# Cross-attention and expert layer on one core: the expert phase written out as a straight program of 136 slots in place of a hardware loop of eight slots a turn

## What is computed

```
x = x + attention(layernorm(x), ctx, ctx)     # causal linear attention, 16 heads, elu+1 features
x = x + ffn(layernorm(x))
ffn: h = relu(x @ W1 + b1); logits = h @ W2 + b2; sel = argmax(softmax(logits))   # 8 experts
     out[token] = x[token] @ expert_W[sel] + expert_b[sel]
```

## Time and profile before

| | us |
|---|---|
| median of three runs | 1158.4 |
| the three runs | 1156.0, 1158.4, 1158.63 |
| span of the profiled execution | 1158.5 |
| of it the second phase, from the first row load (961.3) | 197.2 |
| of it from the first to the last output DMA's issue on POOL | 184.5 |

### The profile page before, as it was taken

One profiled execution on the slowest core, in us unless ns is written; L12 is line 12 of the kernel. 1 busy time (PEld: TensorE's weight loads), 2 busy tenths in 40 slices (PEclk: granted clock), 3 DMA queues, 4 the chain that ended last, 5 costly groups with the idle time before them and its releaser, 6 DMA issues.

```text
span 1158.5 us, 39374 instructions
## 1 busy us (share of the span) xinstructions
PE 1044.3 (90%) x15828; PEld 727.5 (63%) x15829; DVE 843.8 (73%) x1739; ACT 562.7 (49%) x945; POOL 587.0 (51%) x682
## 2 busy tenths in 40 slices
PE   2989999999999999999999999999999626999996
PEld 1666666666666666666667666666667414666664
DVE  2688887887888887878878788888877643555554
ACT  2544544454555544554455545445444114666664
POOL 4144444544444455554555444544444444777766
PEclk9989999999999999999999999999999857999999
DMA  3823333333333333333334333333322014666664
GB/s 104 241 75 93 94 93 94 93 93 93 94 93 95 97 97 97 101 101 100 107 104 120 97 93 93 93 93 93 93 76 76 30 51 138 193 190 184 195 185 135
DMA packets 88601, 127.11 MB, mean 110 GB/s; under 512 B 13693, under 2 KB 67584, under 8 KB 88320
## 3 DMA queue, kind: packets, MB, share of 16 engines
q1 hardware_dynamic: 75392, 89.98, 30.1%
q0 software_dynamic: 13056, 34.90, 7.9%
HBM read 73.03 MB, written 36.06 MB: 94 GB/s over the span
## 4 chain that ended last, share of the span: by engine, by line
PE 23%; issue 23%; POOL 18%; DMA 13%; SPq 7%; ACT 5%; DVE 4%; DVEq 0%; POOLq 0%; ACTq 0%
DMA x_res<-in_x 8%; PE b_a L808 8%; POOL buckets L409 7%; PE b_b L1014 6%; SPq L338 5%; POOL x_res L433 3%; DMA stage<-buckets 2%; DMA out<-stage 2%; PE b_b L855 2%; PE b_a L1005 2%; ACT x2n L494 2%; POOL row L419 2%; PE b_a L803 2%; PE b_b L813 2%; ACT x2T L506 1%
## 5 line engine op out<-in xcount | busy, mean ns | idle before, releaser
L581 DVE TENSOR_TENSOR stage<-b_s,causal 128x1024 f32<-128x1024 f32 x192 | 226.1, 1219 | 47.6 <-PE b_s L835 37.1
L461 POOL DMA_INDIRECT out<-stage x136 | 136.6, 1005 | 59.2 <-issue 30.2
L409 POOL DMA_INDIRECT buckets<-row,place x128 | 140.8, 1100 | 34.6 <-issue 34.6
L1014 PE MATMUL b_b<-we_sb,x3T 128*128 x544 | 150.5, 400 | 0.0
L808 PE MATMUL b_a<-xnT,wq_sb 128*128 128x512 f32 x256 | 128.0, 624 | 7.4 <-ACT x2T L506 5.1
L539 ACT ACTIVATE x3n<-stage 128x256 f32<-128x256 f32 x136 | 81.5, 599 | 88.4 <-DMA stage<-buckets 83.8
L813 PE MATMUL b_b<-wo_sb,attT 128*128 128x256 f32 x512 | 121.4, 391 | 2.4 <-DVE attT L681 2.4
L494 ACT ACTIVATE x2n<-row 128x256 f32<-128x256 f32 x128 | 66.5, 590 | 115.5 <-POOL row L425 115.5
L407 POOL TENSOR_TENSOR onehots<-onehots,onehot 128x32 bf16<-128x32 bf16 x32 | 7.8, 244 | 223.6 <-DVE place L614 223.6
L808 PE MATMUL b_a<-ctxT,wk_sb 128*128 128x512 f32 x256 | 118.4, 605 | 1.8 <-ACT pos L480 1.8
L813 PE MATMUL b_b<-wv_sb,ctxT 128*128 128x256 f32 x512 | 119.0, 385 | 0.0
(11 more groups left out here) (119 smaller groups left out, 1954.4 us busy)
## 6 DMA issues: line engine op xcount, KB each, us to landing
stage<-buckets SPq DMA_DIRECT2D x136, 130.0 KB, 2.2
x_in<-in_x SPq DMA_DIRECT2D x32, 512.0 KB, 5.1
ctxT<-in_ctx SPq DMA_DIRECT2D x32, 512.0 KB, 6.3
qsel<-qp SPq DMA_DIRECT2D x256, 64.0 KB
x_res<-in_x SPq DMA_DIRECT2D x32, 512.0 KB, 7.3
out<-stage POOLq DMA_INDIRECT x136
we_sb<-in_L_ffn_expert_W SPq DMA_DIRECT2D x8, 256.0 KB, 6.0
buckets<-row,place POOLq DMA_INDIRECT x128
```

What stands on the lines that cost most here:

```text
L409: pool.indirect_dma_start(buckets, bass.IndirectOffsetOnAxis(place[:, slot(route), t:t + 1], 0), row[:, slot(route), t, :], None).then_inc ...
L461: pool.indirect_dma_start(out.rearrange("t p n -> (t p) n"), bass.IndirectOffsetOnAxis(rows2[:, r, TOKEN:TOKEN + 1].bitcast(U32), 0), sums ...
L581: dve.tensor_tensor(dst.rearrange("p g h s q -> p g (h s) q"), b_s[:, :, 256 * t:256 * t + 256].rearrange("p g (a q) -> p g a q", q=C), ca ...
L1014: last = pe.matmul(b_b[:, h, 0:D], x3T[:, h, P * k:P * k + P], we_sb[:, k, bass.ds(e, 1), :], start=(k == 0), stop=(k == KC - 1))
```

## The change

`slot_schedule` no longer emits a loop. It goes through all 138 steps and writes each out, with numbers in place of registers for turn and ring place. `begin` is still called ahead of every eighth step, so the table loads stay, 17 or 18 on an engine. First phase, tiles, rings, DMAs and the order of the steps are as before. Lines below the function move up by six in the changed file.

```diff
         def slot_schedule(eng, step, begin=lambda first, how_many: None):
-            begin((0, -2), RING)
-            for j in range(RING):
-                step(*((0, j - k) if j - k >= 0 else None for k in range(3)))
-            with eng.Fori(1, SLOTS // RING, 1) as i:
-                begin((i, -2), RING)
-                for v in range(RING):
-                    step(*((i, v - k) for k in range(3)))
-            begin((SLOTS // RING, -2), 2)
-            for j in range(SLOTS, SLOTS + 2):
-                step(*((j // RING, j % RING - k) if j - k < SLOTS else None for k in range(3)))
+            for j in range(SLOTS + 2):
+                if j % RING == 0:
+                    begin((j // RING, -2), RING if j < SLOTS else 2)
+                step(*(((j - k) // RING, (j - k) % RING) if 0 <= j - k < SLOTS else None for k in range(3)))
```

## The result

The straight program takes 1163.1 us (median of 20 runs, 1157.6 to 1168.5); the kernel before took 1158.5 beside it (20 runs, 1154.6 to 1162.6). The ratio is **1.0043**, with a 95% interval of 1.0030 to 1.0056: slower by some 5 us. Forecast was 1156.4, with a range up to 1160.0.

What follows compares the result with a forecast made beforehand. POOL's output pace of 1.29 us was taken as the second phase's floor, leaving 10.3 us above it to win. Forecast: 1158.5 - 2.1 (turns) - 0.5 (SP's loads) + 0.5 (fetch) = 1156.4 us, range 1152.8 to 1160.0.

Steps and rivals of the forecast that it cites:

- Floor: POOL's outputs in the second phase: steady pace of 1.29 us, 135 steps making 174.2, plus 0.98 for the last.
- Slack: Circle from output landing through load and engines to POOL's issue: 8.36 us against 9.03 for seven outputs, some 0.7 spare.
- The turns: First slot of each loop turn: product 0.51 us earlier without the branch, winning 2.1 us at seven late outputs, bounds 1.4 to 2.3.
- Register instructions and SP's turn (0.5): Second-phase slots: dropped register instructions worth 0; SP's earlier first loads of turns worth 0.5 us, between 0 and 2.1.
- Instruction fetch: Written-out second phase: added instruction packets delay row loads or outputs, costing 0.5 us, bounds 0 to 4.
- three signs: Signs of error: pace under 1.29, "issue" idle of a microsecond or more outside table loads, median row-load landing over 2.5 us.
- The stall of 2.6 and the long issues: POOL's stall of 2.6 us at 1121 and long output issues totalling 2.5 us: both stay, untouched by the change.
- Rival 3: Second phase slower: twenty-five packets at 0.5 us each delay row loads, carried by the circle to POOL; 1168.4, chance 0.07.
- Rivals 1 and 2: Turn gain taken back elsewhere, 1158.0 to 1158.5, chance 0.19; or late outputs elsewhere vanish too, 1154.1 or 1151.5, chance 0.13.
- Rival 4: Second-phase loop was fetched again each turn, so 16 waits of 1.2 us go: 1139, chance 0.01.

Runs made afterwards that it cites:

- pe_loop: Kernel before with the second phase of SP, ACT, DVE and POOL written out, PE keeping its loop: 1159.4 us beside 1159.9, ratio 1.0001.
- pe_straight: Kernel before with the second phase of PE alone written out, the other engines keeping the loop: 1165.7 us beside 1159.9, ratio 1.0048.
- ring_10: Changed (written-out) kernel with rings ten places deep in place of eight and table loads every ten slots: 1156.9 us, 0.9979 of the kernel before.
- pe_64_again: Kernel before with PE alone given a loop of 64 slots and two turns, repeated on a quiet chip: 1164.5 us beside 1159.5, ratio 1.0052.
- loop_ring_10_loads_of_8: Kernel before with rings of ten, a ten-slot loop and each turn's table load split into eight and two: 1193.6 us beside 1189.2, ratio 1.0047.
- loop_ring_10_again: Kernel before with rings of ten and a loop of ten slots, repeated on a quiet chip: 1160.6 us beside 1159.5, ratio 1.0009.
- ring_10_loads_of_8_again: Written-out kernel with rings of ten and eight-register table loads every eighth slot, repeated: 1152.0 us beside the kernel before's 1159.8, ratio 0.9936.
- loop_20_ring_10: Kernel before with rings of ten and a twenty-slot loop, table loads starting at multiples of four words: 1150.6 us beside 1159.8, ratio 0.9933.

## Why the prediction was wrong, and where it was right

**Floor: right. Slack: right in kind.** The pace stays at 1.29, in the changed kernel and in every other one, and the floor of 175.1 for the stretch is real: one kernel came to 177.2. That the ring's circle sets the excess, with little slack, is shown by the rings of ten. The 0.7 itself was too large, as told below.

**The turns: right in the profile.** At slot 38 it reads as forecast (timeline; the product starts 0.51 behind the copy, where it was 1.09 in the earlier trace rows, and DVE idles for 0.42 ahead of its bias, where it was 0.98):

```profile
1017.41 0.36 ACT L541 ACTIVATE x3T<-b_a 128x256 f32<-128x256 f32 x1
...
1017.92 1.12 PE L1008 MATMUL b_b<-we_sb,x3T 128*128 x4
...
1018.65 0.43 DVE L777 TENSOR_TENSOR stage<-stage,bias_e 128x256 f32<-128x256 f32 x1 [0.42 <-issue]
```

Over all 17 table loads the product starts 0.50 to 1.19 behind its copy, 0.63 in the median, where it was 0.58 to 1.33 and 1.06 before; I had named 0.6 to 0.8. By the measure of the prediction, idle time of 0.45 or more, four first outputs of a turn came late where seven had, two by 0.15 and two, behind q8 packets, by 2.65 and 0.68. What the 2.1 us are worth in time no run shows alone, since PE's turns can't be written out without its packets.

**Register instructions and SP's turn (0.5): not seen.** pe_loop has them on four engines and stands at 1.0001, with an interval of 2.5 us to either side, so 0.5 is neither shown nor refuted. Its profile had an excess of 12.5, 2.1 more than before, 0.8 of it from a longer wait at slot 113; none of it was won.

**Instruction fetch: this step failed.** The counts were right, nine packets and sixteen for the 8 to 9 and some 20 forecast. The price was not. I took 0.5 us in all, with 4 as the upper bound. The change lost 5 us and had 2.1 to 2.6 to gain, so by the medians the fetches cost some 7 to 7.6 us, and pe_straight shows that PE's nine packets are the ones that count: 0.8 us each, if its turns gained what I took. Two sentences of the prediction led there. "Each meets one of 16 engines" was no reason for a low price: an output is complete with its last packet, wherever that is, and behind seven of nine fetches an output packet started right at the fetch's end and took over twice the usual time. And "by its full time, less the slack of 0.7" was no upper bound. The fetch took 0.9 to 1.5 us, but its successors were slow too, so those outputs landed after 4.0 to 4.6 us in place of 2.8. The slack of 0.7 was itself too large, since its sum began with a quick landing of 2.39: with the 2.8 that the page of the changed kernel has as the median, it is 0.3. One late landing held up the two or three loads behind it too, and PE, kept waiting, fell to its lower clock once. The evidence for the low end was the first phase, with a packet every 8 us. But nothing there shows a wait of this kind, and I took a phase with other limits as a measure for one that hangs on the latency of small transfers. None of the three signs that I had named for being wrong came either: the pace was 1.29, no engine stood idle for 1 us or more put down to "issue", and the row loads landed in 2.3 us in the median.

**The stall of 2.6 and the long issues stay: right for this kernel.** POOL stood for 2.58 - 0.30 us at 1128, with the sum ready for 3.44.

**The rivals.** Rival 3 was the right one, with 0.07. Its mechanism is as it stood there: late landings carried by the circle to POOL, though chiefly the outputs landed late, where it names the row loads. Its price of 0.5 for each of 25 packets gave 1168.4; measured are 0.6 to 0.8 for each of nine, and nothing that can be told from zero for the sixteen of 8 KB. Rivals 1 and 2 assume that nothing is added and fall with the fetch. Rival 4 had nothing to act on, as said.

The page "Runtime: NRT & Kernel Launch" of the Trainium skill, in its section on instruction fetch mechanics, calls the cost of going over into the next block of instructions mostly hidden. The trace agrees for PE itself, whose idle time in this phase is put down to rows that it waits for. For the kernel as a whole it disagrees: nine such packets cost pe_straight 5.6 us.

## What to carry to other kernels

Writing a loop out buys the branch and pays in instruction packets. Where a phase is bound by bandwidth or by an engine with slack, that costs nothing; where a ring is closed by the landings of small transfers with under 1 us of slack, each 16 KB packet may cost most of a microsecond. So count the packets of the engine with the most instructions, and compare the slack with the whole delay that one gives, successors too. Deepen the ring before touching the program: two more places were worth some 8 us here, 2.5 of them by covering a stall, once the table loads had been put at multiples of four words. Written out or as a loop, the kernel then takes the same time within what the runs can tell.

## What the runs showed of the hardware

- A 16 KB instruction packet took 0.9 to 1.5 us in the changed kernel and in pe_straight, and up to 1.9 in ring_10. In the changed kernel the output packet that started at its end took 0.36 to 0.51 us in place of 0.16 behind seven of nine. Behind copies of 16372 bytes that was seen after none of 17 and three of 34.
- PE ran a loop of 64 slots, five packets long, a second time without fetching it again (pe_64_again).
- A load of eight registers from a table took 0.6 to 0.8 us from a word that is a multiple of four, and 1.9 to 2.3 from word 20i + 10; a load of two took 0.55 from words 20i + 8 and 20i + 18 alike (loop_ring_10_loads_of_8).
- PE's granted clock fell from 1.0 to 0.5 for 3.4 us while it stood idle for some 2.4 us behind a load of ten from word 20i + 10, at four of the six such loads inside the loop of loop_ring_10_again.
- At slot 113 POOL's output issue comes 3.39 us or more behind its addition in all 19 traces. It costs POOL 1.9 to 3.4 us in the eight traces with rings of eight from quiet chips, 1.3 in loop_ring_10_again, 0.2 in ring_10, and nothing in ring_10_loads_of_8_again and loop_20_ring_10, where the addition is early enough. The cause is open.
- On two chips DVE begins 30 to 41 of 136 additions 0.6 to 4 us after their inputs are ready, and the same kernel takes some 1190 us in place of 1159. The cause is open.
